# One projection tile moved across a chunk border, and the split of the low-rank factors placed anew, in a Mamba-2 plus feed-forward kernel

## The reference, cut to what matters

```python
def ref(x, ...):                                    # x: (2, 512, 512)
    x = x + attn(layernorm(x), ...)
    return x + ffn(layernorm(x), ...)

def attn(u, in_proj_w, ...):                        # a Mamba-2 block: 8 groups of 16 heads of 64
    proj = u @ in_proj_w.T
    gate, xBC, dt = ...                             # per group: 8 gate tiles and 10 conv tiles of 128 rows
    xBC = silu(depthwise_conv4(xBC) + conv_b)
    y = ssd(hs, A, Bm, Cm, D, dt, dt_bias)          # chunked scan with a state carried along the sequence
    g = y * silu(gate)
    g = g * rsqrt(mean(g*g over a group) + eps) * norm_w
    return g @ out_w.T

def ffn(x, w1, w3, w2, A1, B1, A3, B3, A2, B2):     # 512 -> 1376 -> 512, each weight with a rank 16 part
    lin = lambda v, w, a, b: v @ w.T + (v @ a.T) @ b.T * 2.0
    return lin(silu(lin(x, w1, A1, B1)) * lin(x, w3, A3, B3), w2, A2, B2)
```

## Time and profile before

| what | us |
|---|---|
| median of three runs | 1792.4 |
| lowest and highest | 1792.03 and 1793.68 |
| the profiled execution, its time | 1792.14 |
| the profiled execution, its span | 1790.4 |
| TensorE busy in the span | 1761.6 |

### The profile page before, as it was taken

How to read it: one execution, slowest core, us unless ns; L and a number is a source line. 1 busy time by engine, 2 the same in 40 slices (tenths; PEclk the granted TensorE clock), 3 DMA queues, 4 the chain that set the end, 5 groups by cost and what they waited for, 6 DMA issues and landing times.

```text
span 1790.4 us, 27417 instructions
## 1 busy us (share of the span) xinstructions
PE 1761.6 (98%) x9815; PEld 1429.5 (80%) x9815; DVE 1208.0 (67%) x2083; ACT 1154.2 (64%) x2192; POOL 1079.5 (60%) x1011
## 2 busy tenths in 40 slices
PE   7999999999999999999999999999999999999999
PEld 5778887888878888888788878888788878787887
DVE  7796677757685768667875767576866688564323
ACT  5877577766756677757776676667766766643421
POOL 4475657666666557565756666656766565755520
PEclk9999999999999999999999999999999999999999
DMA  4643435334543344343533454334344353344201
GB/s 153 178 120 115 118 112 159 92 111 124 157 118 112 112 133 123 110 124 110 164 94 117 113 157 118 112 115 148 101 116 117 112 166 92 105 118 136 78 20 47
DMA packets 122038, 211.61 MB, mean 118 GB/s; under 512 B 24240, under 2 KB 28976, under 8 KB 121904
## 3 DMA queue, kind: packets, MB, share of 16 engines
q1 hardware_dynamic: 121904, 209.87, 40.4%
HBM read 205.09 MB, written 4.72 MB: 117 GB/s over the span
## 4 chain that ended last, share of the span: by engine, by line
PE 89%; DVE 8%; issue 2%; ACT 1%; POOL 0%; DMA 0%; DVEq 0%; POOLq 0%; ACTq 0%
PE bank L1594 15%; PE bank L1596 15%; PE bank L1595 15%; PE bank L1663 7%; PE bank L1705 6%; PE bank L1706 6%; PE bank L1707 6%; PE bank L1693 5%; PE bank L1676 4%; DVE ow_l L1303 3%; PE bank L1639 3%; PE bank L1921 1%; PE bank L1922 1%; PE bank L1920 1%; DVE bcT L1297 1%
## 5 line engine op out<-in xcount | busy, mean ns | idle before, releaser
L660 POOL TENSOR_TENSOR w_l<-w_raw,w_h 128x512 fp32r<-128x512 f32 x288 | 380.5, 1325 | 470.6 <-ACT w_h L836 470.6
L1594 PE MATMUL bank<-x_h,w_h 128*128 128x512 f32 (+1 forms) x1328 | 531.3, 400 | 5.7 <-DVE bcT L1297 3.0
L1596 PE MATMUL bank<-x_h,w_l 128*128 128x512 f32 (+1 forms) x1328 | 519.1, 391 | 0.0
L1595 PE MATMUL bank<-x_l,w_h 128*128 128x512 f32 (+1 forms) x1328 | 518.1, 390 | 0.0
L1297 DVE SCALAR_TENSOR_TENSOR x_ch<-bank,par,x_ch 128x511 f32<-128x511 f32 (+2 forms) x384 | 287.5, 749 | 107.7 <-ACT x_ch L854 98.6
L889 ACT ACTIVATE decay<-decay,cols 128x128 f32<-128x128 f32 x1024 | 316.2, 390 | 0.8
L1594 PEld LDWEIGHTS bank<-x_h,w_h 128*128 128x128 f32 (+1 forms) x1328 | 249.4, 188 | 57.6 <-issue 4.6
L1596 PEld LDWEIGHTS bank<-x_h,w_l 128*128 128x128 f32 (+1 forms) x1328 | 248.8, 187 | 54.9
L1595 PEld LDWEIGHTS bank<-x_l,w_h 128*128 128x128 f32 (+1 forms) x1328 | 249.6, 188 | 48.5
L854 ACT ACTIVATE x_ch<-bank,par 128x512 f32<-128x512 f32 x128 | 99.3, 776 | 224.2 <-PE bank L1596 224.2
L1326 DVE TENSOR_TENSOR decay<-decay,bank 128x512 f32<-128x512 f32 x256 | 172.3, 682 | 92.4 <-ACT decay L889 92.3
(11 more groups left out here) (149 smaller groups left out, 2588.0 us busy)
## 6 DMA issues: line engine op xcount, KB each, us to landing
w_raw<-in_wp SPq DMA_DIRECT2D x288, 256.0 KB, 2.9
decay<-cum_scratch SPq DMA_DIRECT2D x256, 256.0 KB, 4.0
ec<-ecum_scratch SPq DMA_DIRECT2D x96, 256.0 KB, 6.3
ow_raw<-in_ow SPq DMA_DIRECT2D x64, 256.0 KB, 4.8
w_raw<-in_w SPq DMA_DIRECT2D x48, 256.0 KB, 2.7
acc<-in_x SPq DMA_DIRECT2D x8, 256.0 KB, 4.4
out<-acc SPq DMA_DIRECT2D x8, 256.0 KB, 2.0
cols<-cols_scratch SPq DMA_DIRECT2D x16, 96.0 KB, 3.1
```

The lines of the kernel that those rows point to most:

```text
L660: pool.tensor_tensor(w_l[:, s, :], w_raw[:, s, :], w_h[:, s, :].bitcast(F32), ALU.subtract).then_inc(wl_ready, 1)
L1594: pe.matmul(dst, wh, xh, start=(opens and k == 0), stop=False)
L1595: pe.matmul(dst, wh, xl, start=False, stop=False)
L1596: last = pe.matmul(dst, wl, xh, start=False, stop=(k == len(terms) - 1 and not more))
```

## The change

Five things move, and no arithmetic is added or left out.

1. The last projected tile (17) leaves chunk 3 and stands in chunk 4, behind `new_state` and ahead of `norm_transpose(1, 3)`. Its drain on ScalarE (`gate`) moves along.
2. In chunk 3, `match` goes ahead of tile 16 and `turn_x` behind it. In chunk 4, `turn_x` goes behind `norm_transpose(1, 3)` and `match`.
3. The subtraction for the low part of `lb` goes from GpSimd to VectorE (`lb_low`), and `up(0)` no longer waits for it at its start: its last matmul does.
4. `lb_raw` lies in `hidden_0b` and no longer in slots 3 to 5 of the weight ring. So `lb` is loaded at once, and the feed-forward weights 3 and 4 follow directly, without a wait for the split of `lb`.
5. The order on VectorE and GpSimd in chunk 3 is written out anew, `norm_apply(1, 3)` goes ahead of `add_state` in chunk 4, and ScalarE splits `la` ahead of the first feed-forward weight.

The diff, cut to its core:

```diff
-        lb_raw = w_raw[0:STACK, 3:WRING, :].rearrange("p s n -> p (s n)")[:, 0:FFN]
+        lb_raw = hidden_0b[0:STACK, :, :].rearrange("p m t -> p (m t)")[:, 0:FFN]
...
                 sp.wait_ge(g_ready, LAST * CHUNKS + SC)
                 sp.dma_start(lora[:, 0:LA_COLS], la_in).then_inc(lora_loaded, 16)
-                for i in range(3):
+                sp.dma_start(lb_raw, lb_in).then_inc(lora_loaded, 16)
+                for i in range(WRING - 1):
                     load_up(i)
-                sp.wait_ge(pj_done, up_no(0))
-                sp.dma_start(lb_raw, lb_in).then_inc(lora_loaded, 16)
...
                 if k == SC:
-                    sp.wait_ge(lb_l_ready, 1)
-                    for i in range(3, WRING):
-                        load_up(i)
+                    load_up(WRING - 1)
...
                     pool.tensor_tensor(la_l[:, :], la_raw, la_h[:, :].bitcast(F32), ALU.subtract).then_inc(la_l_ready, 1)
-                    pool.wait_ge(lb_h_ready, 1)
-                    pool.wait_ge(la_l_ready, 1)
-                    pool.wait_ge(inv_ready, CHUNKS + SC)
-                    mid = slice(2 * RANK, 4 * RANK)
-                    pool.tensor_tensor(lbT[mid, :], lb_raw[mid, :], lbT[mid, :].bitcast(F32), ALU.subtract).then_inc(lb_l_ready, 1)
-                    pool.wait_ge(lb_l_ready, 1)
...
+                    if last and c == SC - 1:
+                        mask(gn, kn, 0)
+                        inverse_root(g, k - 1)
+                        mask(gn, kn, 1)
+                        mask(gn, kn, 2)
+                        gT_low(g, k)
+                        mask(gn, kn, 3)
+                        norm_inverse(1, c - 1)
+                        square_sum(g, k)
+                        weigh_x(gn, kn)
+                        inverse_root(g, k)
+                        continue
...
                 if k == SC:
-                    up_high(0)
                     act.wait_ge(lora_loaded, 32)
                     act.activation(la_h[:, :], la_raw, ACT.Copy).then_inc(la_h_ready, 1)
+                    up_high(0)
                     act.activation(lb_raw, lb_raw, ACT.Copy, scale=LORA_SCALE).then_inc(lb_scaled, 1)
                     act.wait_ge(lb_scaled, 1)
                     act.activation(lbT[0:STACK, :], lb_raw, ACT.Copy).then_inc(lb_h_ready, 1)
+                    gate(LAST, 1, TILES - 1)
...
+            def lb_low():
+                mid = slice(2 * RANK, 4 * RANK)
+                dve.wait_ge(lb_h_ready, 1)
+                dve.tensor_tensor(lbT[mid, :], lb_raw[mid, :], lbT[mid, :].bitcast(F32), ALU.subtract).then_inc(lb_l_ready, 1)
...
                 if k == SC:
                     add_skip(LAST, k)
+                    norm_apply(1, k - 1)
                     add_state(LAST, k)
-                    norm_apply(1, k - 1)
                     gated(LAST, k)
                     norm_low(1, k - 1)
                     scale_x(LAST, k + 1)
                     scale_across(LAST, k + 1)
+                    lb_low()
                     low_low(0)
...
                 if k == 1 and c == SC - 1:
-                    pe.wait_ge(gate_done, gate_no(2 * GROUPS - 1, CT))
+                    pe.wait_ge(gate_done, gate_no(2 * GROUPS - 1, CT) - 1)
...
                 if k == SC:
-                    turn_x(LAST, k + 1)
+                    project(LAST, 1, TILES - 1)
                     norm_transpose(1, k - 1)
                     match(LAST, k + 1)
+                    turn_x(LAST, k + 1)
                     across(LAST, k + 1)
                     pe.wait_ge(la_l_ready, 1)
+                    pe.wait_ge(gate_done, gate_no(2 * GROUPS - 1, CT))
                     low_product(0)
                     out_half(LAST, k, 0)
+                    up(t, False)
                     pe.wait_ge(lb_l_ready, 1)
-                    pe.wait_ge(low_l_ready, 2)
-                    up(t)
+                    up_lora(t)
                     up(t + 1)
...
-                    turn_x(gn, kn)
-                    match(gn, kn)
+                    if last and c == SC - 1:
+                        match(gn, kn)
+                        projects(tiles[1:-1])
+                        turn_x(gn, kn)
+                    else:
+                        turn_x(gn, kn)
+                        match(gn, kn)
```

More of the change, by code:

```diff
@@ L783, in body @@
                         continue
-                    late = last and c == SC - 1
+                    if last and c == SC - 1:
[10 more added lines that the diff above has]
+                        continue
                     if k > 0:
@@ L797, in body @@
                             mask(gn, kn, q)
[L798 to L803, removed]
                     if c < SC - 1:
@@ L1133, in body @@
                             norm_high(1, 2)
-                        tile(tiles[1:])
+                        tile(tiles[1:-1] if last else tiles[1:])
                         if k == CHUNKS - 1:
@@ L1522, in body @@
                         mean_square(*before)
+                    gated(g, k)
                     if late:
@@ L1525, in body @@
                         norm_low(1, 1)
-                    gated(g, k)
+                        accumulate(*before)
+                        norm_moments(1, 2)
+                        scale_x(gn, kn)
+                        norm_apply(1, 2)
+                        for q in range(QUARTERS):
+                            scores(gn, kn, q)
+                        mean_square(g, k)
+                        norm_low(1, 2)
+                        accumulate(g, k)
+                        norm_moments(1, c)
+                        continue
                     taps_of(tiles[:1])
-                    scale_x(gn, kn)
                     if k == 0:
@@ L1540, in body @@
                         norm_moments(1, 1)
-                    if late:
-                        norm_moments(1, 2)
-                        scores(gn, kn, 0)
-                        norm_apply(1, 2)
-                        for q in range(1, QUARTERS):
-                            scores(gn, kn, q)
-                        mean_square(g, k)
-                        norm_low(1, 2)
-                        accumulate(g, k)
-                        norm_moments(1, c)
-                        continue
                     taps_of(tiles[1:2])
@@ L1875, in body @@
                         projects(tiles[:1])
-                    turn_x(gn, kn)
-                    match(gn, kn)
+                    if last and c == SC - 1:
[5 more added lines that the diff above has]
+                        match(gn, kn)
                     if c == SC - 1:
-                        projects(tiles[1:])
+                        if not last:
+                            projects(tiles[1:])
                         out_half(g, k, 0)
```

## The result

The changed kernel takes 1783.28 us (median of five executions, 1782.43 to 1784.69) against 1792.41 (five, 1792.03 to 1793.68): 9.1 us faster, a ratio of 0.9948 with an interval of 0.9933 to 0.9962. The profiled execution took 1784.69, with a span of 1782.9. It is the slowest of the five, which matters further down.

What follows compares the result with a forecast made beforehand. TensorE, busy 1761.6 of 1790.4 us, was taken to bound the kernel. Removed 5.86 less added 1.52 gave a gain of 4.34 us (range 3.7 to 5.0): 1787.8 for the profiled execution, median 1788.1; overall range 1786.4 to 1790.4.

Steps and rivals of the forecast that it cites:

- The loss at the border: Chunks 3 to 4, last group: 5.86 us lost before `turn_x`, before `norm_transpose`, to low clock, before `up(0)`; all won back.
- The parts for `xn` and the clock: Chunk 4: 2.23 us waited before `norm_transpose` for `xn`, and 1.70 us lost to low clock behind it; both removed.
- the 1.70 for the clock: Chunk 4, behind the two gaps: 4.17 us for 2.47 us of work at 1.2 GHz; expected back with no long gap.
- The new waits: Chunk 3, added on TensorE: 0.30 us before `out_half`, 0.23 before `norm_transpose(1, 2)`, 0.84 before `square_total`.
- No wait before `turn_x` and the transposes of chunk 4: Chunk 4: tile 17 and the new order remove the gaps of 1.64 us before `turn_x` and 2.23 before `norm_transpose`.
- `lb_low` costed at nothing: Chunk 4, VectorE: the 1.58 us subtraction mostly passes during `low_product`, with 2.55 us to spare before `up(0)`'s last matmul.
- The third rival: Chunk 4: `lb_low` keeps losing to GpSimd, `up(0)`'s last matmul 1.7 us late; gain 2.6 us; chance 0.04.
- rivals 1 and 5: Clock falls all the same, gain 2.64 us, chance 0.10; clock falls before `square_total` and stays low, 5.2 slower, chance 0.03.
- Rival 2: Chunk 3: waits smaller, `xn` gets in ahead, sum of squares not held up; gain 5.2 to 5.7 us; chance 0.11.
- rival 4: Chunk 3 or 4: another wait exceeds its upper bound; gain near 3.3 us, time 1788.8; chance 0.10.
- 1.64: Chunk 4: the wait before `turn_x`, 3.46 us less 1.82 for `new_state`, counted as removed.
- 1.52: All added costs: chunk 3 waits 0.30, 0.23, 0.84, its new order 0.03, and 0.12 for tile 17's start in chunk 4.

Runs made afterwards that it cites:

- the subtraction alone: Kernel before with only the subtraction for the low part of `lb` moved to VectorE, no tile moved: 1788.92 us against 1793.0.
- the missed edit alone: Kernel before with only the first two `ow_low` put ahead of `scale_x` in each group's first chunk: 1788.11 us against 1793.0.

## Why the prediction was right and wrong, by its own steps

- **The step that failed** is the sentence that leads into the part on chunk 3: "Up to the end of tile 15 in chunk 3, at 1520.74, nothing moves on TensorE." It put at nothing a hunk of the diff that runs in every group. The two `ow_low` that go ahead of `scale_x` are in a branch for the first chunk of every group. They take away 0.6 us in each of seven groups and 0.7 (0.9 less 0.2) in group 0, 4.9 by the lists of waits and 4.8 from start to start; alone they measured 4.9 us. The rival that would have held the result wasn't on the list. The trace before had it in plain sight, as the second largest entry of TensorE's waits. The prediction read waits only around the place that the change is named after.
- **The loss at the border**, 5.86 us in four parts, was read rightly. The parts for `xn` and the clock together, 3.93, went with the subtraction alone, which measured 4.1 (3.80 at the border). But the 1.70 for the clock is what one execution lost: with the missed edit alone the same border, with the same two gaps, took 1.2 more.
- **The new waits.** Before `out_half` forecast 0.30; start to start it is 1521.59 - 1520.42 - 0.88 = 0.29. Before the transposes of chunk 3: 0.23, and 1524.52 - 1521.59 - 2.72 = 0.21; the meeting of `xn` with GpSimd went as in the earlier trace rows, 1.50 us. Before `square_total`: 0.84, and 1525.65 - 1524.52 - 0.44 = 0.69, mis-sized by 0.15, since GpSimd's sum took 2.68 behind the inverse (1522.92 to 1525.60) and not 2.83.
- **Missed at the border**: `gated` of chunk 4 waits for all gates of its unit, and the last of them now comes behind tile 17. VectorE stood 1.82 us, and `across` began 1537.48 - 1536.08 - 0.88 = 0.52 late. The rule for a moved step, to ask who waits for its drain, was applied to `low_product` and not to `gated`. So the border gave 4.0 and not 4.3: 0.52 less for this, 0.15 more for the wait before `square_total`, and hundredths in the rest.
- **No wait before `turn_x` and the transposes of chunk 4, tile 17 at 1536 to 1539** (here 1532.1 to 1535.3, everything being 3.4 us and more ahead), **the last matmul of `up(0)` not late**: all as forecast.
- **`lb_low` costed at nothing**: right. It took 1.99, not 1.58, as GpSimd's `gT_l` ran until 1541.0, and GpSimd's two masks then took 2.57 instead of 1.23 in return. The third rival, that it keeps losing, didn't happen: it waited for one instruction. The Trainium skill's rule ("SBUF — State Buffer", "Who interferes with whom"), that a VectorE instruction with two SBUF inputs contends with a GpSimd instruction that reads SBUF, agrees with both rows within 0.15 us: `lb_low` began 0.55 before `gT_l` ended, and 0.55 + 1.58 = 2.13; the masks began 1.48 before `lb_low` ended, and 1.48 + 1.23 = 2.71.

```profile
1538.60 2.40 POOL L681 TENSOR_TENSOR gT_l<-sgT,gT_h 128x1024 fp32r<-128x1024 f32 x1 [3.42 <-ACT gT_h L898]
1540.96 2.57 POOL L663 TENSOR_SCALAR_AFFINE_SELECT decay<-decay 128x512 f32<-128x512 f32 x2
```

- **The clock** stayed up, as forecast, with the three waits of chunk 3; rivals 1 and 5 didn't happen. Rival 2, smaller waits in chunk 3, came true only by its 0.15; rival 4 named a longer wait in chunk 3 or 4, and the one of chunk 4 (0.52) did come, but it was less than the 1.0 that the rival reckoned with.
- **The reason given for the gain was incomplete in another way**: the sum credited the tile with 1.64 and charged 1.52 for the waits around it. That they cancel was in the numbers, but not said; the runs without the tile show it, 30.7 against 30.5 us.

## What to carry to other kernels

List every hunk of a diff with the loop that it stands in, before reading the trace: a line in a body that runs in all groups outweighs ten lines in the one place that the change is named after. Then hold the page's list of waits of the bounding engine against the diff, entry by entry, and ask of each whether a moved line stands in front of its releaser. A tile put into a gap wins only if the steps that lost their cover, and the steps that wait for its drain, are moved with it; here these waits took nearly all of what the tile won. And where an edit is worth a few us, compare the traces at the place itself, from start to start, before the totals.

## What the runs showed of the hardware that wasn't expected

- A gap of TensorE of 1.47 us with no second one close behind left the clock at 1.00 in the three kernels without the moved tile that had the subtraction on VectorE. With both gaps, 1.47 and 2.05, and the transposes between them, it fell, in both kernels that had them, and the price varied. In the kernel before, `low_product` came 4.17 us after the transposes. In the kernel with the missed edit alone the low clock went on into `low_product`, and the same stretch took 4.82 (1537.22 to 1542.04); its windows (stretch, PE, PEld, DVE, ACT, POOL, clock, DMA):

```profile
1536.00:1538.00 2.00, 0.78 (x4) 0.79 (x5) 2.00 (x3) 0.00 (x0) 1.80 (x3) 0.61 0.27 51
1538.00:1543.00 5.00, 5.00 (x23) 4.74 (x22) 3.43 (x6) 3.69 (x6) 3.31 (x4) 0.50 0.46 154
```

- A wait of 0.2 to 0.3 us before a matmul can be missing from the list of waits, since the modelled length of the matmul before it, 0.39 us where the steps are 0.23, covers it; only steps from start to start show it. In two places here it came in seven groups, 1.8 and 2.0 us in all.
- Late loads of decay rows cost the profiled execution of the changed kernel 1.3 us in chunk 7 of two groups, and its first 20 us were 0.8 longer than those of its repetition (the same four matmuls began at 16.97 and at 16.91 and the transposes behind them at 18.68 and 17.84), in an execution 1.4 us above the median. Why the start differs isn't shown. One trace is then a poor measure of a gain of this size, and the position where the difference arises is the better one.
